# The tile step of a gated two-layer block: p transposed by DMA, output products one step later, norms on ScalarE

## What is computed

```python
x = x + jnp.tanh(g_xattn[0]) * _L0_xattn_ref(_layernorm(x), fside, ctx_1024)
x = x + jnp.tanh(g_ffn[0]) * _L0_ffn_ref(_layernorm(x), gate_w, gate_b, val_w, val_b, out_w, out_b)
x = x + jnp.tanh(g_xattn[1]) * _L1_xattn_ref(_layernorm(x), ctx_1024, Wq, bq, Wk, bk)
x = x + jnp.tanh(g_ffn[1]) * _L1_ffn_ref(_layernorm(x), router_w, down_w, up_w)
```

```python
def bit_linear(x, w, b):
    scale_x = 127.0 / jnp.clip(jnp.max(jnp.abs(x), axis=-1, keepdims=True), 1e-05, None)
    x_dq = jnp.clip(jnp.round(x * scale_x), -128.0, 127.0) / scale_x
    gamma_w = jnp.clip(jnp.mean(jnp.abs(w)), 1e-05, None)
    w_dq = jnp.clip(jnp.round(w / gamma_w), -1.0, 1.0) * gamma_w
    return jnp.einsum('bsd,hd->bsh', x_dq, w_dq) + b
gate = jax.nn.silu(bit_linear(x, gate_w, gate_b))
val = bit_linear(x, val_w, val_b)
return bit_linear(gate * val, out_w, out_b)
```

## Time and profile before

| | |
|---|---|
| median of 3 runs | 607.82 us (607.14 to 610.41) |
| the profiled execution: its time, its span | 608.18 us, 606.3 us |
| TensorE matmuls busy | 487.4 us (80%), 2534 instructions |
| VectorE busy | 460.4 us (76%), 1063 |
| ScalarE busy | 331.4 us (55%), 558 |
| POOL busy | 209.0 us (34%), 294 |
| chain that ended last | PE 32%, DVE 13%, POOL 7%, issue 5% |
| mean granted TensorE clock | 0.923 of full speed |

### The profile page before, as it was taken

The page is one execution under the profiler, slowest core; times in us unless marked ns, Lnnn a source line. Parts: engine busy times, 40 slices in busy tenths (PEclk is TensorE's granted clock), DMA queues, the critical chain, the costliest instruction groups (busy, mean ns, idle before and its releaser), DMA issues.

```text
span 606.3 us, 8564 instructions
## 1 busy us (share of the span) xinstructions
PE 487.4 (80%) x2534; PEld 256.8 (42%) x2534; DVE 460.4 (76%) x1063; ACT 331.4 (55%) x558; POOL 209.0 (34%) x294
## 2 busy tenths in 40 slices
PE   1546887757756758779999999999999999999964
PEld 1435544434433425234444544454454445445522
DVE  4678798998994689456688788778877887886653
ACT  2558759839748649445454544554454455446510
POOL 2344245535634346521144214313431432241121
PEclk9965979979978888789999999999999999999995
DMA  8885003011004400000000000000000000000000
GB/s 317 242 327 174 1 5 105 1 69 35 0 1 157 156 0 18 1 0 1 1 2 18 18 0 17 17 17 0 17 17 17 0 17 17 0 18 18 17 17 35
DMA packets 21718, 28.69 MB, mean 47 GB/s; under 512 B 8376, under 2 KB 10680, under 8 KB 21184
## 3 DMA queue, kind: packets, MB, share of 16 engines
...
## 4 chain that ended last, share of the span: by engine, by line
PE 32%; DVE 13%; POOL 7%; issue 5%; ACT 1%; DVEq 1%; POOLq 0%
PE p_out L1622 9%; PE p_gate L1615 7%; PE p_val L1615 6%; POOL ey L1373 3%; POOL rstd L161 3%; DVE stats L201 3%; DVE beat L1467 3%; PE p_out L1640 2%; PE p_tr L1603 2%; PE p_out L1655 2%; PE p_gate L1612 2%; DVE u L1402 1%; DVE x_all L1418 1%; POOL rstd L160 1%; PE p_val L1612 1%
## 5 line engine op out<-in xcount | busy, mean ns | idle before, releaser
L1550 ACT ACTIVATE silu_g<-p_gate,bcol 128x512 f32<-128x512 f32 x64 | 44.0, 687 | 86.9 <-PE p_gate L1615 79.8
L160 POOL TENSOR_TENSOR rstd<-mv,ln_eps 128x1 f32<-128x1 f32 x48 | 10.0, 209 | 228.2 <-DVE mv L203 227.7
L1655 PE MATMUL p_out<-out_t,p_t 128*128 128x512 bf16 x256 | 66.8, 385 | 1.5 <-ACT p_t L1558 1.4
L1615 PE MATMUL p_gate<-gate_t,q_room 128*128 128x512 bf16 x256 | 67.4, 386 | 0.0
L1402 DVE TENSOR_TENSOR u<-p_val,silu_g 128x512 f32<-128x512 f32 x64 | 44.1, 688 | 30.1 <-PE p_val L1615 28.0
L1615 PE MATMUL p_val<-val_t,q_room 128*128 128x512 bf16 x256 | 66.6, 383 | 0.0
L1554 ACT ACTIVATE p<-u,bcol 128x512 f16<-128x512 f32 x64 | 42.7, 714 | 32.3 <-DVE bcol L1412 32.3
L1622 PE MATMUL p_out<-att_t,lt_c 128*128 (+1 forms) x128 | 57.5, 592 | 0.0
L1404 DVE TENSOR_REDUCE mu<-u 128x1 f32<-128x512 f32 x64 | 43.9, 686 | 2.2
L1418 DVE SCALAR_TENSOR_TENSOR x_all<-p_out,tanh_g,x_all 128x512 f32 (+1 forms) x32 | 23.9, 747 | 23.9 <-PE p_out L1622 19.6
L1558 ACT ACTIVATE p_t<-p_tr 128x512 bf16<-128x512 f16 x64 | 36.3, 593 | 7.4 <-PE p_tr L1646 4.9
...
## 6 DMA issues: line engine op xcount, KB each, us to landing
...
out_dram<-x_all SPq DMA_DIRECT2D x16, 256.0 KB, 2.0
...
x_all<-in_x SPq DMA_DIRECT2D x1, 2048.0 KB, 10.4
```

Source lines behind the costliest of these rows:

```text
L1550: nc.scalar.activation(silu_g[:, c % 2, :], p_gate[:, c % 2, :], ACT.Silu, scale=col(CG)).then_inc(silu_done, 1)
L1615: last = nc.tensor.matmul(bank[:, c % 2, :], x_t[:, k * P:(k + 1) * P], w_t[m][:, k, cols], start=False, stop=k == KD - 1)
L1655: last = nc.tensor.matmul(p_out[:, 0, :], p_t[:, k * P:(k + 1) * P], w_t[2][:, k, :], start=k == 0, stop=k == KH - 1)
```

## The change

It has five parts, all in the second part of the kernel except for the hand-over.

1. **p is transposed by DMA.** `b_spread` and `b_transposed` go. SP issues four `dma_start_transpose` per tile, one for each 512 columns, from `p16` (p) straight to `p_t`, each with a semaphore of its own. Nothing takes the 1536 off then, so `p_t` and the output weights become f16 with the offset still in p, and `b_output` begins with one product of a constant matrix of -1536 with `out_sums`, the sum of the weights' sixteen row blocks, which `column_sums` makes once, in step 0, by sixteen products with the identity.
2. **The output products of tile i-1 stand in step i**, behind chunk 0; `b_add`, `c_statistics`, and further behind `c_add` and `d_statistics` move with them.
3. **x has two slots**: `x_t` of tile i+1 is made in step i, in PSUM bank 0 of `p_tr`.
4. **The three norms move to ScalarE**: POOL makes `shift` = -mean x rstd in a third operation, and ScalarE computes rstd x + shift. The norm of tile i+1 is made in step i, not two steps ahead, and only tile 0 is prepared in the first part.
5. **The rank** takes one subtraction and one comparison against a table of 0 and -1.25e-38 where it took a comparison, an equality, a product and a sum.

The loop is gone: all sixteen steps are written out, on every engine. Stores of x share SP's list with the transposes.

```diff
-               out_raw[:, :].bitcast(BF16).rearrange("p (k d) -> p k d", k=KH)]
+               out_raw[:, :].bitcast(F16).rearrange("p (k d) -> p k d", k=KH)]
...
-        x_t = q_room[:, at + AUG // 2:at + AUG].bitcast(BF16)
+        xaug = q_room[:, at:at + P // 2].bitcast(BF16)
+        at += P // 2
+        x_t = [q_room[:, at + r * AUG // 2:at + (r + 1) * AUG // 2].bitcast(BF16) for r in range(2)]
...
+            need(pool, last_norm, n)
+            link = Chain(pool, chain, n, 2)
             link(nc.gpsimd.tensor_tensor(rstd[:, s:s + 1], mv[:, s, 1:2], ln_eps[:, 0:1], ALU.add))
-            nc.gpsimd.tensor_tensor(rstd[:, s:s + 1], rstd[:, s:s + 1], half_neg[:, 0:1], ALU.pow).then_inc(rstd_ready, 1)
+            link(nc.gpsimd.tensor_tensor(rstd[:, s:s + 1], rstd[:, s:s + 1], half_neg[:, 0:1], ALU.pow))
+            nc.gpsimd.tensor_scalar(shift[:, s:s + 1], mv[:, s, 0:1], rstd[:, s:s + 1], -1.0, ALU.mult, ALU.mult).then_inc(rstd_ready, 1)
...
-        def norm(s, n, dst):
-            return nc.vector.tensor_scalar(dst[:, :], tile_of(n), mv[:, s, 0:1], rstd[:, s:s + 1], ALU.subtract, ALU.mult)
+        def norm(act, s, n, dst, rstd_ready, done):
+            act.wait_ge(rstd_ready, n + 1)
+            nc.scalar.activation(dst[:, :], tile_of(n), ACT.Identity, bias=shift[:, s:s + 1], scale=rstd[:, s:s + 1]).then_inc(done, 1)
...
-            nc.scalar.activation(x_t[:, 0:D], tr_16[1][:, 0:D], ACT.Copy, bias=-ROUND16)
-            nc.scalar.activation(x_t[:, D:AUG], tr_h[1][:, D:AUG], ACT.Copy).then_inc(xt_ready, 1)
+            nc.scalar.activation(x_t[n % 2][:, 0:D], tr_16[0][:, 0:D], ACT.Copy, bias=-ROUND16)
+            nc.scalar.activation(x_t[n % 2][:, D:AUG], tr_h[0][:, D:AUG], ACT.Copy).then_inc(xt_ready, 1)
...
+                def p_transpose(n, c):
+                    sp.wait_ge(b_p16, HC * n + c + 1)
+                    if c == 0:
+                        need(sp, b_mm, n)
+                    cols = slice(c * 512, (c + 1) * 512)
+                    sp.dma_start_transpose(out=p_t[:, cols].rearrange("p (k r) -> p k r", r=P), in_=p16[:, cols]).then_inc(pt_ready[c], 16)
+
+                def store(n):
                     sp.wait_ge(d_x, n + 1)
                     sp.dma_start(rows[bass.ds(n, 1)].rearrange("n p d -> p (n d)"), tile_of(n)).then_inc(stored, 16)
+
+                for i in range(NT):
+                    for c in range(HC):
+                        p_transpose(i, c)
+                    if i >= 3:
+                        store(i - 3)
+                for n in range(NT - 3, NT):
+                    store(n)
...
-                    nc.vector.tensor_tensor(beat[:, :, :], rival, own, ALU.is_gt)
-                    link(nc.vector.tensor_tensor(tie[:, :, :], rival, own, ALU.is_equal))
-                    link(nc.vector.tensor_tensor(tie[:, :, :], tie[:, :, :], tri[:, :, :], ALU.mult))
-                    link(nc.vector.tensor_tensor(beat[:, :, :], beat[:, :, :], tie[:, :, :], ALU.add))
+                    link(nc.vector.tensor_tensor(beat[:, :, :], rival, own, ALU.subtract))
+                    link(nc.vector.tensor_tensor(beat[:, :, :], beat[:, :, :], tri[:, :, :], ALU.is_gt))
...
-                def step(i, with_c, with_d, with_e, with_q, with_q2):
+                def step(i):
                     b_link = Chain(dve, b_chain, i, HC + 3)
-                    if with_c:
+                    if i >= 2:
+                        c_add(i - 2)
+                        d_statistics(i - 2)
+                    if i + 1 < NT:
+                        q_statistics(dve, i + 1)
+                    b_link(b_product(i, 0))
+                    if i >= 3:
+                        d_gate(i - 3)
+                    if i >= 1:
+                        b_add(i - 1)
                         c_statistics(i - 1)
-                    if with_d:
-                        d_norm(i - 2)
-                    b_link(b_product(i, 0))
-                    if with_c:
-                        c_norm(i - 1)
-                    for c in range(1, HC):
-                        b_link(b_product(i, c))
+                    if i + 1 < NT:
+                        q_maximum(dve, i + 1)
+                    b_link(b_product(i, 1))
+                    b_link(b_product(i, 2))
+                    if i >= 3:
+                        e_add(i - 3)
+                    b_link(b_product(i, 3))
                     b_scales(i, b_link)
                     b_link.end()
-                    if with_e:
-                        e_add(i - 3)
-                    if with_c:
-                        c_add(i - 1)
-                    if with_q2:
-                        q_statistics(dve, i + 2)
-                    if with_c:
-                        d_statistics(i - 1)
-                    if with_d:
-                        d_link = d_logits(i - 2)
-                    if with_q:
+                    if i >= 2:
+                        d_logits(i - 2)
+                    if i + 1 < NT:
+                        dve.wait_ge(b_qs, i + 1)
...
+                def c_norm(n):
+                    need(act, c_tr, n)
+                    norm(act, 1, n, ln_c, c_rstd, c_ln)
+
+                def d_norm(n):
+                    need(act, d_tr, n)
+                    norm(act, 2, n, ln_d, d_rstd, d_ln)
...
-                def b_transposed(n, c):
-                    act.wait_ge(b_tr, HC * n + c + 1)
-                    nc.scalar.activation(p_t[:, c * 512:(c + 1) * 512], tr_16[(c + 1) % 2][:, 0:512], ACT.Copy, bias=-ROUND16).then_inc(pt_ready, 1)
-
-                def step(i, with_c, with_d, with_e, with_q, with_q2):
+                def step(i):
                     act.wait_ge(q_cols, i + 1)
                     b_gate(i, 0)
-                    if with_e:
+                    if i >= 2:
+                        d_norm(i - 2)
+                    if i + 1 < NT:
+                        q_norm(act, i + 1)
+                    b_gate(i, 1)
+                    if i >= 2:
+                        d_transposed(i - 2)
+                    if i >= 3:
                         e_transposed(i - 3)
-                    b_gate(i, 1)
                     b_gate(i, 2)
-                    if with_d:
-                        d_transposed(i - 2)
-                    if with_c:
+                    if i >= 1:
+                        c_norm(i - 1)
+                    if i + 1 < NT:
+                        q_scaled(act, i + 1)
+                    if i >= 1:
                         c_transposed(i - 1)
                     b_gate(i, 3)
-                    if with_q:
-                        q_scaled(act, i + 1)
+                    if i + 1 < NT:
+                        x_transposed(act, i + 1)
                     act.wait_ge(b_qs, i + 1)
-                    for c in range(HC - 1):
-                        b_scaled(c)
-                    b_transposed(i, 0)
-                    b_transposed(i, 1)
-                    b_scaled(HC - 1)
-                    if with_d:
+                    for c in range(HC):
+                        b_scaled(i, c)
+                    if i >= 2:
                         d_hidden(i - 2)
-                    b_transposed(i, 2)
-                    b_transposed(i, 3)
-                    if with_q:
-                        x_transposed(act, i + 1)
-
-                schedule(act, step)
+                    if i == 0:
+                        copy(out_sums[:, :], p_out[:, 1, :], sums_mm, 1, sums_ready)
...
+                def column_sums():
+                    for k in range(KH):
+                        last = nc.tensor.matmul(p_out[:, 1, :], ident_16[:, :], w_t[2][:, k, :], start=k == 0, stop=k == KH - 1)
+                    last.then_inc(sums_mm, 1)
+                    pe.wait_ge(offset_made, 1)
+                    pe.wait_ge(sums_ready, 1)
+
+                def b_output(n):
+                    need(pe, c_x, n)
+                    nc.tensor.matmul(p_out[:, 0, :], neg_offset[:, :], out_sums[:, :], start=True, stop=False)
+                    for c in range(HC):
+                        pe.wait_ge(pt_ready[c], 16 * (n + 1))
+                        for k in range(c * (KH // HC), (c + 1) * (KH // HC)):
+                            last = nc.tensor.matmul(p_out[:, 0, :], p_t[:, k * P:(k + 1) * P], w_t[2][:, k, :], start=False, stop=k == KH - 1)
+                    last.then_inc(b_mm, 1)
+
+                def step(i):
                     pe.wait_ge(xt_ready, i + 1)
                     b_chunk(i, 0)
-                    if with_e:
+                    if i >= 1:
+                        b_output(i - 1)
+                    b_chunk(i, 1)
+                    if i >= 2:
+                        spread(0, ln_d, d_ln, i - 2, d_tr)
+                    if i >= 3:
                         e_spread(i - 3)
-                    b_chunk(i, 1)
                     b_chunk(i, 2)
-                    if with_e:
-                        pe.wait_ge(d_at_copied, i - 2)
-                    if with_d:
```

(29 more changed lines are left out.)

188 lines of the change are left out of this document (82 added, 106 removed).

## The result

The changed kernel takes **599.4 us** (median of 4 runs, 598.9 to 600.0) against 608.7 for the kernel before on the same chip: ratio 0.984, 95% interval 0.982 to 0.986. It is 1.6% faster, clear of the noise, and inside the range, but it gains 9 us where 19 were forecast. The profiled execution took 600.0 us for a span of 598.2, 8.1 us less than the span before.

The account below looks back on a forecast made before the run. The prediction took TensorE, nearly always busy in steps 4 to 13, to set the pace. Its terms for the steady steps and the ends summed to -19.3 us: 608.2 - 19.3 = 589 us, range 576 to 640.

Parts of the forecast that it names:

- the steady step: Tile steps 4 to 13: TensorE's step falls from 20.95 to 19.6 us, 1.33 less each, -13.3 us in all.
- the new wait: In each steady step TensorE waits 0.65 us for `ln_c`, whose norm stands behind chunk 2's silu on ScalarE.
- The waits that went: TensorE's old waits in a step, for `a_d`, chunk 2's bank, copies of p and x's slot: 1.3 us together.
- the wait at the step's start: TensorE's wait of 0.4 us before a step, put down to x's one slot, to go with a second.
- the price G: Time one DMA transpose holds SP's queue: taken as 1.2 us, between 0.6 and 8.0, with landing 1.4 us behind it.
- 4(G - 1.2): Growth of each step in us for G above 1.2, as the four DMA transposes run behind one another.
- rival B: DMA transposes cost a part of the gain: G between 1.25 and 1.45 us, 592 to 605 us; chance 0.15.
- It puts the kernel exactly on the edge of its slack: With G at 1.2 us the four transposes just cause no stall before the output products; hence the uneven range.
- steps 0 to 2 and 14 were written out before and show no other gaps, so 0: Writing the program out for all sixteen tiles, where a loop ran over eleven, was costed at 0 us.
- the ends: Step 0 -4.9, steps 1 to 3 -1.5, -0.7, -1.0, step 14 -1.0, step 15 and after +4.7, -0.2, -1.4 us.
- About -1.4: Behind the last attention product, tile 15's router product no longer stands behind tile 14's rank: about 1.4 us saved.
- Rivals A and C: A: transposes become the bound, G above 1.55, chance 0.29. C: late norms hold up silus, 604 to 608 us, chance 0.02.

## Why the prediction was right and wrong

**Right: the steady step.** 20.95 - 0.88 - 1.3 + 0.22 + 0.65 = 19.6 was measured as 19.68. The transposes of p were worth 0.88 (0.87 in the run with them put back), the offset product 0.22, and the new wait stood where it was said. Its size was 0.79 by the starts and not 0.65: `ln_c` starts 1.39 + 0.59 behind the chunk, as said, but the norm takes 0.80, where 0.71 was taken from a cast, and 0.06 passes until TensorE starts. That the sum still comes out is in part luck. The waits that went were 1.45 us and not 1.3 (the step without the new wait is 18.84): the one for `a_d` was read as 0.39 from its brackets and is 0.54 by the starts (392.08 + 0.87 to 393.49). The two errors have opposite signs.

**Right by number, wrong by cause: the wait at the step's start.** The prediction has it that it "goes with the second slot of x". With one slot it is gone as well. The likely reason is the order: the attention product (3.5 us) now stands between the transposes of x and the next chunk, where four output products (0.87) stood. No run tests that alone.

**Right: the price G, nearly.** 1.28 us where 1.2 was taken as "twice a plain issue", and 2.5 us to landing behind the issue where 2.6 was assumed (G + 1.4). That 1.28 cost the steady step nothing is luck again: by the prediction's 4(G - 1.2) each step would have grown by 0.32 us, and the time would be 594 us, in rival B's range. The first transpose goes out 1.5 us before the step ends and not 1.4, and each lands 1.2 behind its hold and not 1.4, so the last lands at +4.83 and is wanted at +4.89. The trace of before could not give it, and what the size is made of, a price for each instruction and none for its blocks, was only seen in the runs with other widths. The Trainium skill, "VectorE: DVE Perf Modes", section "The three transpose paths", gives 1309 ns for a DMA transpose of 128x128. By these runs that is about what an instruction costs, whatever it holds; the 5.2 us (845 us in all) came from multiplying the figure by four blocks, and an instruction of eight blocks took 1.30.

**Wrong: the step "It puts the kernel exactly on the edge of its slack".** This is the step that failed. The prediction saw the edge, kept it for the range, and costed it at nothing in the sum. On the edge, any delay is paid. Of the 11.2 us that are missing, 7.1 are late transposes: 1.4 in step 2, 1.2 in step 3, 2.0 in steps 6 and 13, 1.0 in step 15, each from the rows' number and 0.16, and 1.5 behind step 15, where the last group of output products begins at +6.3 and the prediction had it at +4.8 (it counted the rest of the waits there). All but step 2's stand beside a code load that met transposes under way. No term stood for such a delay. The nearest one, for writing the program out, was set to 0 with a reason that did not bear on it: "steps 0 to 2 and 14 were written out before and show no other gaps, so 0". They showed none because nothing in those steps depended on a DMA. The steady steps of the written-out program are no longer than the loop's (19.66 to 19.71 us in both); what unrolling did was to put 7 more loads of 16 KB and 6 more of 8 KB on the DMA engines that the transposes had just begun to use. Its share is only a part: with TensorE's loop back, waits in the list fall from 6.3 to 3.2 us, and the waits of steps 2, 3 and 15 stay, where steps 2 and 15 were written out before too. The slack is the rest: with it the loads that remain cost nothing, 6.1 us by the medians. Rival B had the outcome (592 to 605 us), but by a G above 1.25 that is paid in every step; what happened is a late transpose now and then.

**Wrong: the ends.** The addition of tile 15 was put at +5.9 us behind the step's end and came at +7.4, by the last transpose, beside a code load. There is a wait in front that the prediction did not have, 0.85 us: the output products use the bank of PSUM that the attention product of tile 14 has just filled, and must wait for VectorE's addition (the row at 564.47); elsewhere chunk 0 stands between the two. It cost nothing, since the last transpose was later still. "About -1.4" behind the attention product was -0.6: the router product no longer waits, as said, but the norm of d there has a third root operation (0.27) and takes 0.81 on ScalarE where VectorE took 0.55, about 0.5 us that the sum held for the norm of c alone. Step 1 missed by 2.1 us: 1.7 of it (19.01 against 17.33) is the lower clock, in an execution that had the fall, behind a wait of 1.83 us that the change itself puts in front of the step and that the sum has in step 0 alone. The 2 us that are left are spread over the steady steps (0.08 each) and steps 1 and 2, whose parts were estimated with less care than the steady step's.

**Rivals A and C** did not come: TensorE waits for transposes in six places of the program and not in every step, and no silu waits for POOL's `shift`.
